# A reordered, reformulated first batch norm and eight more TensorE filler matmuls in a four-layer fused kernel

## The reference, cut to what matters

```
def _gn(v, G=32, eps=1e-05):      # mean and variance over groups of 4 channels
    ...
    return ((g - m) / jnp.sqrt(s + eps)).reshape(v.shape)

def _L1_conv_ref(x, conv_w, bn1_gamma, bn1_beta, bn2_gamma, bn2_beta, prelu_a):
    res = x
    h = _batchnorm(x, bn1_gamma, bn1_beta)      # (x - m) * rsqrt(v + EPS) * gamma + beta
    h = jnp.sign(h)
    sw = _weight_scale(conv_w)
    bw = jnp.sign(conv_w) * sw
    h = conv(h, bw, 3x3, padding 1, 16 groups)
    h = _batchnorm(h, bn2_gamma, bn2_beta)
    h = h + res
    return jnp.where(h > 0, h, prelu_a * h)
```

## Time and profile before

| what | value |
|---|---|
| median of 3 runs | 76.61 us |
| the three runs | 76.24, 76.61, 78.25 us |
| profiled execution, first to last instruction (span) | 75.0 us |
| busy: PE, DVE, ACT, POOL | 61.9, 51.8, 39.5, 37.7 us |
| mean granted TensorE clock, profiled execution | 0.970 |

### The profile page before, as it was taken

The page is one execution under the profiler, slowest core; times in us unless marked ns, Lnnn a source line. Parts: engine busy times, 40 slices in busy tenths (PEclk is TensorE's granted clock), DMA queues, the critical chain, the costliest instruction groups (busy, mean ns, idle before and its releaser), DMA issues.

```text
span 75.0 us, 1268 instructions
## 1 busy us (share of the span) xinstructions
PE 61.9 (83%) x371; PEld 50.9 (68%) x371; DVE 51.8 (69%) x179; ACT 39.5 (53%) x114; POOL 37.7 (50%) x81
## 2 busy tenths in 40 slices
PE   3993889799999999069999439949998999999930
PEld 2762778498999776046788238838775879899810
DVE  3919859674689979802262994999999998743530
ACT  5103884758945000092003889976548597977410
POOL 6605999889604547900003975999991334200000
PEclk9999999999999999975799999999999999999997
DMA  0692000000000000000000000000000000002222
GB/s 4 162 395 81 0 0 0 0 0 4 0 0 9 4 0 0 0 4 0 0 9 0 0 0 0 0 0 0 0 0 0 0 0 0 4 9 70 70 70 70
DMA packets 1415, 1.81 MB, mean 24 GB/s; under 512 B 128, under 2 KB 1152, under 8 KB 1408
## 3 DMA queue, kind: packets, MB, share of 16 engines
q1 hardware_dynamic: 1408, 1.73, 7.0%
HBM read 1.20 MB, written 0.52 MB: 23 GB/s over the span
## 4 chain that ended last, share of the span: by engine, by line
PE 33%; DVE 23%; issue 18%; POOL 13%; DMA 6%; ACT 3%; SPq 1%; POOLq 0%; ACTq 0%
DMA x<-in_x 6%; PE bank L1259 4%; DVE t L750 3%; PE bank L1324 3%; POOL gn_rstd L321 3%; PE bank L1347 3%; PE bank L1405 3%; POOL dw_rest L398 3%; PE bank L1385 3%; PE bank L1283 3%; DVE x L853 2%; DVE dw_acc L961 2%; POOL x_res L414 2%; PE bank L1270 2%; PE bank L1365 2%
## 5 line engine op out<-in xcount | busy, mean ns | idle before, releaser
L321 POOL TENSOR_TENSOR gn_rstd<-gn_var_eps,minus_half 128x1 f32<-128x1 f32 (+1 forms) x14 | 9.1, 651 | 13.5 <-DVE gn_var_eps L744 13.4
L1324 PE MATMUL bank<-x,dw_diag 128*128 128x256 f32 x40 | 9.5, 385 | 2.2 <-DVE x L943 2.2
L1180 PE MATMUL bank<-warm 128*128 128x256 bf16 x67 | 10.3, 314 | 1.2 <-POOL warm L306 1.2
L1324 PEld LDWEIGHTS bank<-x,dw_diag 128*128 128x128 f32 x40 | 7.3, 189 | 3.4 <-DVE x L943 2.5
L1180 PEld LDWEIGHTS bank<-warm 128*128 128x128 bf16 x67 | 7.4, 113 | 2.9 <-POOL warm L306 1.2
L1296 PE MATMUL bank<-signs,conv_blocks 128*128 128x256 bf16 x36 | 5.9, 338 | 2.6 <-ACT signs L524 2.6
L1296 PEld LDWEIGHTS bank<-signs,conv_blocks 128*128 128x128 bf16 x36 | 4.2, 118 | 4.4 <-issue 3.0
L524 ACT ACTIVATE signs<-res,bn_shift,bn_scale 128x256 bf16<-128x256 f32 x4 | 2.2, 598 | 8.2 <-DVE bn_shift L913 8.2
L919 DVE BATCH_NORM_STATS2 bn_stats<-bank 128x6 f32<-128x256 f32 x4 | 1.7, 432 | 5.4 <-PE bank L1296 5.4
L321 POOL TENSOR_TENSOR bn_rstd<-bn_var_eps,minus_half 128x1 f32<-128x1 f32 x2 | 1.2, 602 | 8.4 <-DVE bn_var_eps L929 7.8
L531 ACT ACTIVATE bn_out<-bank,bn_shift,bn_scale 128x256 f32<-128x256 f32 x4 | 2.0, 558 | 6.4 <-DVE bn_shift L913 6.4
(11 more groups left out here) (151 smaller groups left out, 169.3 us busy)
## 6 DMA issues: line engine op xcount, KB each, us to landing
out<-x SPq DMA_DIRECT2D x4, 128.0 KB, 1.7
late_params<-in_late SPq DMA_DIRECT2D x1, 404.5 KB, 4.8
x<-in_x SPq DMA_DIRECT2D x1, 384.0 KB, 4.1
early_params<-in_early SPq DMA_DIRECT2D x1, 258.0 KB, 4.3
x<-in_x SPq DMA_DIRECT2D x1, 128.0 KB, 2.0
```

The source lines that it names most:

```text
L321: return nc.gpsimd.tensor_tensor(out_ap, in_ap, minus_half[:, 0:n], ALU.pow)
L1180: nc.tensor.matmul(bank[:, 0:N], warm[:, 0:C], warm[:, :], start=True, stop=True)
L1324: ins = nc.tensor.matmul(dw_ps[b], dw_diag[:, tap, :], xs[2][:, b, dy:dy + H, dx:dx + W], start=(tap == 0), stop=(tap == PE_TAPS - 1))
```

## The change

Six edits, all around the first batch norm:

- VectorE forms the tiny numbers of the first batch norm before it writes the normalised images 1 to 3, and the order among them changes: `gn_mean_sq(1, 3)` goes before `group_out(1, 2)`, `bn1_e2_eps` goes before `bn1_mean`.
- GpSimd's root becomes a standard deviation (`pow` with +0.5). ScalarE's sign takes `gamma` as its scale and `beta * sd - gamma * mean` as its bias, which has the same sign as the batch norm's result since `sd` is positive. `gamma * mean` is made while the root is taken. So one VectorE instruction follows the root where two did.
- The root stands ahead of all four `x1_res_out` in GpSimd's queue.
- `x1_res_out(0)` now waits until the shift is made, so the four sums run under the convolution.
- TensorE gets `keep_warm(8)` between `valid_taps(8)` and `conv(0)`.
- The second batch norm's helpers are written out on their own and do what they did.

```diff
@@ GpSimd: constants and roots
+            nc.gpsimd.memset(plus_half[:, :], 0.5)
...
-            def bn_root(i):
-                pool.wait_ge(bn_var_ready, i + 1)
-                root(bn_rs[:, i:i + 1], bn_ve[:, i:i + 1]).then_inc(bn_rstd_ready, 1)
+            def bn1_root():
+                pool.wait_ge(bn_var_ready, 1)
+                nc.gpsimd.tensor_tensor(bn1_sd[:, :], bn_ve[:, 0:1], plus_half[:, :],
+                                        ALU.pow).then_inc(bn_rstd_ready, 1)
...
             def x1_res_out(b):
+                if b == 0:
+                    pool.wait_ge(bn_shift_ready, 1)
                 pool.wait_ge(t_ready[1], b + 1)
@@ GpSimd: the order
             gn_root(1, 0)
-            x1_res_out(0)
             gn_root(1, 1)
             gn_root(1, 2)
             gn_root(1, 3)
+            bn1_root()
+            x1_res_out(0)
             x1_res_out(1)
-            bn_root(0)
             x1_res_out(2)
             x1_res_out(3)
-            bn_root(1)
+            bn2_root()
@@ ScalarE: sign_out
-                                     bias=bn_shift[:, 0:1], scale=bn_scale[:, 0:1]).then_inc(sign_ready, 1)
+                                     bias=bn_shift[:, 0:1],
+                                     scale=lp[:, LC["bn1_gamma"]]).then_inc(sign_ready, 1)
@@ VectorE: new helpers
+            def bn1_e2_eps():
+                settle("bn1_e2")
+                step(nc.vector.tensor_scalar(bn1_e2[:, 1:2], bn1_e2[:, 0:1], EPS, None, ALU.add),
+                     "bn1_e2_eps")
...
+            def bn1_gamma_mean():
+                settle("bn_mv", 0)
+                step(nc.vector.tensor_tensor(bn1_gm[:, :], bn_mv[:, 0, 0:1], lp[:, LC["bn1_gamma"]],
+                                             ALU.mult), "bn1_gm")
+
+            def bn1_shift_out():
+
+                dve.wait_ge(bn_rstd_ready, 1)
+                settle("bn1_gm")
                 nc.vector.scalar_tensor_tensor(
+                    out=bn_shift[:, 0:1], in0=bn1_sd[:, :], scalar=lp[:, LC["bn1_beta"]],
+                    in1=bn1_gm[:, :], op0=ALU.mult, op1=ALU.subtract).then_inc(bn_shift_ready, 1)
@@ VectorE: the order
             gn_aggr(1, 3)
+            gn_mean_sq(1, 3)
             group_out(1, 2)
-            gn_mean_sq(1, 3)
             group_var(1, 2)
             group_out(1, 3)
             group_var(1, 3)
-            norm1(1)
             bn1_mean_sq()
+            bn1_e2_eps()
             bn1_mean()
             bn1_var()
+            bn1_gamma_mean()
+            norm1(1)
             norm1(2)
+            bn1_shift_out()
             norm1(3)
-            bn_scale_out(0)
-            bn_shift_out(0)
             bn2_stats(0)
@@ TensorE: the order
             valid_taps(8)
+            pe.wait_ge(exp_ready, 2 * B)
+            keep_warm(8)
             conv(0)
```

More of the change, by code:

```diff
@@ L80, in build @@
         minus_half = sb("minus_half", [C, B])
+        plus_half = sb("plus_half", [C, 1])
         bias_rows = sb("bias_rows", [C, 2, C])
@@ L169, in build @@
         bn_rs = sb("bn_rstd", [C, 2])
+        bn1_sd = sb("bn1_sd", [C, 1])
+        bn1_gm = sb("bn1_gamma_mean", [C, 1])
         bn_scale = sb("bn_scale", [C, 2])
@@ L405, in dw_scale_out, with bn2_root @@
                                         ALU.mult).then_inc(dw_scale_ready, 1)
-            def bn_root(i):
-                pool.wait_ge(bn_var_ready, i + 1)
-                root(bn_rs[:, i:i + 1], bn_ve[:, i:i + 1]).then_inc(bn_rstd_ready, 1)
+            def bn1_root():
+                pool.wait_ge(bn_var_ready, 1)
+                nc.gpsimd.tensor_tensor(bn1_sd[:, :], bn_ve[:, 0:1], plus_half[:, :],
+                                        ALU.pow).then_inc(bn_rstd_ready, 1)
+            def bn2_root():
+                pool.wait_ge(bn_var_ready, 2)
+                root(bn_rs[:, 1:2], bn_ve[:, 1:2]).then_inc(bn_rstd_ready, 1)
             def x1_res_out(b):
+                if b == 0:
+                    pool.wait_ge(bn_shift_ready, 1)
                 pool.wait_ge(t_ready[1], b + 1)
@@ L878, in bn1_mean_sq @@
                      "bn1_sq")
+                settle("bn1_inv")
                 settle("bn1_sq")
@@ L888, in bn1_mean @@
                     op0=ALU.mult, op1=ALU.mult, accum_out=bn_mv[:, 0, 0:1]), "bn_mv", 0)
-                settle("bn1_e2")
-                step(nc.vector.tensor_scalar(bn1_e2[:, 1:2], bn1_e2[:, 0:1], EPS, None, ALU.add),
-                     "bn1_e2_eps")
             def bn1_var():
                 settle("bn1_e2_eps")
+                settle("bn_mv", 0)
                 mean = bn_mv[:, 0, 0:1]
@@ L898, in bn1_var, with bn2_scale_out, bn2_shift_out @@
                     op1=ALU.subtract, reverse1=True).then_inc(bn_var_ready, 1)
[L900 to L912, removed]
-                nc.vector.scalar_tensor_tensor(
-                    out=bn_shift[:, i:i + 1], in0=bn_mv[:, i, 0:1], scalar=bn_scale[:, i:i + 1],
-                    in1=beta, op0=ALU.mult, op1=ALU.subtract, reverse1=True).then_inc(bn_shift_ready, 1)
+            def bn1_gamma_mean():
+                settle("bn_mv", 0)
+                step(nc.vector.tensor_tensor(bn1_gm[:, :], bn_mv[:, 0, 0:1], lp[:, LC["bn1_gamma"]],
[3 more added lines that the diff above has]
+                settle("bn1_gm")
+                nc.vector.scalar_tensor_tensor(
+                    out=bn_shift[:, 0:1], in0=bn1_sd[:, :], scalar=lp[:, LC["bn1_beta"]],
+                    in1=bn1_gm[:, :], op0=ALU.mult, op1=ALU.subtract).then_inc(bn_shift_ready, 1)
+            def bn2_scale_out():
+                dve.wait_ge(bn_rstd_ready, 2)
+                settle("sw_gamma")
+                step(nc.vector.tensor_tensor(bn_scale[:, 1:2], bn_rs[:, 1:2], sw_gamma[:, :], ALU.mult),
+                     "bn_scale", 1)
+            def bn2_shift_out():
+                settle("bn_scale", 1)
+                nc.vector.scalar_tensor_tensor(
+                    out=bn_shift[:, 1:2], in0=bn_mv[:, 1, 0:1], scalar=bn_scale[:, 1:2],
+                    in1=lp[:, LC["bn2_beta"]], op0=ALU.mult, op1=ALU.subtract,
+                    reverse1=True).then_inc(bn_shift_ready, 1)
             def bn2_stats(b):
@@ L1096, in _ @@
             bn2_var()
-            bn_scale_out(1)
-            bn_shift_out(1)
+            bn2_scale_out()
+            bn2_shift_out()
             h1_out(0)
```

## The result

The changed kernel takes 73.82 us (median of 4 runs, 73.05 to 74.63); the kernel before, now with a fourth run, 76.5 us (76.24 to 78.25). The ratio is 0.9585, with a 95% interval of 0.9542 to 0.9629. It leaves out runs more than 1.5% above the fastest of their kernel; here these are the two changed runs whose mean granted clock was low: 74.43 (0.970) and 74.63 us (0.971), against 73.05 (0.993) and 73.21 us (0.998), and the 78.25 of before. The profiled execution is the one of 73.21 us, with a span of 71.5, so 1.7 us lie around a span.

The account below looks back on a forecast made before the run. The prediction blamed TensorE's 2.61 us wait for the first signs, then a half-clock convolution. An earlier start (1.70) and faster run (1.65), together 3.35, took 76.61 to 73.3 us, range 72.6 to 75.6.

Parts of the forecast that it names:

- Order of the statistics: VectorE's last group statistics: `gn_mean_sq(1, 3)` ahead of `group_out(1, 2)` gains nothing and delays a PSUM bank's release, +0.05 us.
- `norm1(1)` moved behind: VectorE after the last group variance: without this image in between, the instructions up to line 880 start earlier, gain 0.24 us.
- Line 880 freed: VectorE's `bn_products`: away from GpSimd's `x_res` sum it takes 0.15 us where it took 0.63.
- The root: GpSimd's `pow` with +0.5 in the first batch norm: 0.65 us, between 0.5 and 0.75, with no other algorithm expected.
- Images under the root: VectorE while GpSimd takes the root: `norm1(1)` and `norm1(2)`, 0.73 us for two, fit with nothing to spare.
- One instruction instead of two: VectorE behind the root: shift alone takes 0.22 us without a GpSimd sum; the first sign starts 1.70 us earlier overall.
- The clock, 1.65: TensorE in the convolution: fillers keep the clock at 2.4 GHz, so it takes 4.21 us against 5.86, gain 1.65.
- The first rival: The clock falls after the 2.22 us gap behind the convolution instead, costing 1.65 us: time 74.9 us, chance 0.19.
- The second: The median runs of before had no clock fall, so only the earlier convolution start counts: 74.9 us, chance 0.17.
- the dip in the clock shows up somewhere else: Sign of a wrong prediction: TensorE's clock dips elsewhere in the changed kernel's profile, where full clock was expected around the convolution.
- Slower: The clock falls in the 2.22 us gap and stays down through the depthwise stage: 81 us, chance 0.03.
- the change not doing what it says: Fillers do not hold the clock in the convolution and only the chain gains: 74.9 us, chance 0.04.

Follow-up runs that it names:

- the kernel with early fillers: Changed kernel with 51 fillers behind the convolution, old statistics order, all images behind the shift, 6 fillers before the convolution, and 6 not 2 before `other_group_means()`: median 72.75 us.

## Why the prediction was right or wrong

The time came out at 73.82 us against 73.3, and the full-clock runs at 73.05 and 73.21. The two terms were 1.70 and 1.65, and measured 1.48 and 1.60 in the profiles. The missing 0.22 of the chain lie at the order of the statistics (0.08), on the way to the variance (0.08) and at the root (0.07). Point by point:

*What bounds the kernel.* Right. The three odd VectorE instructions waited for GpSimd's sums; undoing the new wait brought 0.67 us back at once.

*Order of the statistics, +0.05 between 0 and +0.15.* Mis-sized, 0.13. In the traces `gn_mean_sq(1, 3)` starts 0.67 us behind the last image's statistics in either order, so being first in the queue gained it nothing. `group_out(1, 2)` moved from 0.56 to 0.81 us behind them, and the matmul of the last group mean from 0.95 to 1.08. That it waited for the bank is inferred: the profile names `gn_mean_sq` as its releaser, which came no later than before.

*`norm1(1)` moved behind.* Right within 0.05: line 880 (895 now) starts 0.81 us behind the last group variance, where it was 1.05 and I had 0.76.

*Line 880 freed.* 0.16 and not 0.63, as forecast. But I let the variance follow the mean's accumulator reading at 0.11 us from its start. It follows at 0.20 (28.40 to 28.60). With the 0.05 above and small differences the other way the variance is 1.37 us behind the last group variance and not 1.29.

*The root, 0.65 between 0.5 and 0.75.* 0.72. No other algorithm: it is 0.55 with VectorE quiet and 0.65 with the images beside it but without `gamma * mean`. That instruction does not run beside the root: it is over at 28.88 and the root starts at 28.89. It does move the images, which start 0.09 us ahead of the root, where it was 0.16 before the change and with the old algebra. Whether this or the exponent under load makes the last 0.07 I did not separate.

*Images under the root.* They fit (0.73 and done at 29.53, the root at 29.61), but not for free, as I had it: they slow the root by 0.17 us. Three meetings of VectorE and GpSimd have a price in the traces: the root beside images takes 0.72 against 0.55, an image behind a started sum 0.91 against 0.41, and a shift behind a started sum 0.67 against 0.22. The Trainium skill (GPSIMD Engine Reference, section 1, Specifications) says that GpSimd's SBUF interfaces are shared with VectorE. The shift has the two SBUF inputs that the statement names; an image has one, and no row tells whether it runs in the two-port mode that it names beside them. At the place where I applied it, `norm1(3)` against the first sum, the image in the profile got in 0.16 us ahead of the sum and took its usual 0.41; one of the four sums took longer, as the row of that line shows:

```profile
L427 POOL TENSOR_TENSOR x_res<-x,res x4: 727/729/840, 29.9 to 32.1; 128x256 f32<-128x256 f32 x4
```

*One instruction instead of two.* I had put scale and shift at 1.36 us going to 0.22. True, but nearly all of that is that no sum stands beside them. The experiments split it: the algebra by itself is worth 0.12 us, the wait 0.44 at the shift alone.

*Eight fillers at no cost.* Right: the convolution starts 0.75 us behind the first sign, as before, and TensorE idles about 0.1 us there (the fillers end at 30.58).

*The clock, 1.65.* The size is right, 1.60. The step that failed is the reason, that with the fillers "the clock should stay at 2.4 GHz": without them it stayed as well, in the execution that was profiled. And it was not the same in all executions: the kernel before has no fall in 18 of 40 further runs, and the changed kernel has one in 5 of 10. The first rival (a later fall) happens in part of the executions: the median of the five upper changed runs is 74.39 us and that of the five lower ones 73.21, so it costs 1.2 us where I had 1.65. The second was wrong about the runs on record, which were fallen ones by their times, but the kernel before does run without a fall, at 74.3 to 74.65 us. I had made these alternatives to the forecast, when they are outcomes of the same two kernels. The median of 73.82 is a mixture of 73.1 and 74.5, and "the dip in the clock shows up somewhere else", which I had named as a sign of being wrong, is what the clocks of 0.970 and 0.971 stand for. That the ratio came out as forecast, 0.9585 against 0.957, is partly luck: all four runs of the kernel before had a fall, by their times, where 18 of 40 later ones had none, and against those the change is worth about 2%.

*Slower, and the change not doing what it says.* Neither came. In the trace with the fall in the depthwise matmuls (8 fillers, old chain) only the first ten suffered; the second ten took 2.40 us again.

## What to carry to other kernels

When a one-column instruction takes three times its usual time, look at what GpSimd does at that moment, and move the bulk work behind the chain; here that was most of 1.5 us, and the algebra only 0.12. Read a dip of the clock in one profiled execution as one outcome among several: ask in how many runs it occurs before its price goes into a sum, and look at every other gap of like length, since closing one leaves the other to decide the median. Here 18 more fillers in the gap that stayed took the upper runs away (none of 22, against 5 of 10), while eight fillers in the gap that the shorter chain had cut to 1.01 us changed nothing in the one profiled execution without them.

## What the runs showed that I had not expected

Around the convolution TensorE was at full clock after 1.01 and 1.74 us of idle time. It was at half clock after 2.61, and after 2.21 in one profile and not in the others; since 18 of 40 runs of the kernel before had no fall, either of its gaps can be passed at full clock. There is also a fall after shorter gaps, early in the kernel, in four profiles: with 8 and with 22 fillers in the old chain, with the old order of statistics, and with the images behind the shift. For the third of them the timeline shows gaps of 0.82 and 1.00 us with few matmuls between, and the stretches behind them show the clock:

```profile
5.76 0.49 PE L1235 MATMUL bank<-early_params 128*128 128x128 f32 x2 [0.82 <-DMA early_params<-in_early]
6.09 0.38 PE L1210 MATMUL bank<-warm 128*128 128x256 bf16 x2
7.47 0.59 PE L1252 MATMUL bank<-gn_mean_sq,group_avg 128*128 128x6 f32 x2 [1.00 <-DVE gn_mean_sq L787]
```

```profile
7.00:8.00 1.00, 0.53 (x3) 0.53 (x3) 0.74 (x6) 1.00 (x4) 0.94 (x4) 0.74 0.00 0
8.00:9.00 1.00, 1.00 (x4) 0.82 (x4) 0.77 (x5) 0.16 (x1) 0.86 (x5) 0.50 0.00 0
```

In that kernel the two runs with 0.976 are 0.55 and 0.61 us above the one with 1.000 (73.25 and 73.31 against 72.70), and 0.14 and 0.20 above the one with 0.995 (73.11), so a fall there costs less than the 1.60 in the convolution. The traces give its price up to the last image's statistics: 20.70 to 20.74 us from the first statistics that wait for the input, in these four, against 20.50 to 20.53 in the ten others, so 0.2 us.

The length of the gaps alone does not decide. The kernel before idled 0.46 and 1.01 us at these two places without a fall; the kernel with the images behind the shift idled 0.44 and 1.00 us, and the clock fell. The executions differ before that. The five fillers that start at 4.2 to 4.5 us took 0.71 to 0.95 us in the four with the fall, and 0.99 to 1.23 us in nine of the others. The tenth is the kernel with early fillers: they took 0.75 us, as in the four, the gaps were 0.26 and 0.57 us, and the clock stayed. So how TensorE began may decide what a later gap does to the clock. No experiment set it, and it stays open.
